# Layer-norm state updated in place, and the last residual add moved from VectorE to GpSimd

## The chip, the core and the metric

The program runs on one core of one Trainium2 chip. The metric is the device time of one execution in microseconds (us); lower is better. The engines are TensorE (PE in the profile), VectorE (DVE), ScalarE (ACT), GpSimd (POOL) and SyncE (SP), which issues most of the transfers. Each engine runs its own instruction list in order, and lists meet only at semaphores.

## The reference, cut to what matters

One decoder layer with layer norm after each residual, float32, on x of shape (8, 128, 256) and a context of the same shape:

```python
x = layernorm(x + attention(x, Wq, Wk, Wv, Wo))          # 16 heads of 128, 4 key/value heads, rotary
x = layernorm(x + long_convolution(ctx, ctx, x, kernel, D))  # pair products of ctx, convolved, times x
x = layernorm(x + gated_attention(x, W_gate, W_qkv))     # 16 heads of 16, top-1 gate picks k and v
```

All three norms are `(x - mean) / sqrt(var + 1e-5)` over the 256 features, with no weights.

## The kernel before, in words

The 8 sequences of 128 tokens each live in SBUF as `x[128, 8, 256]`, one token per partition. The program has two phases.

**Phase A** runs the first attention and the convolutions, in 8 units of four heads and half of the sequences. It ends with `accumulate`, which adds the attention's output into `x`. All of phase A but its last unit is the same in both kernels.

**Phase B** handles the sequences one after another in turns `b = 0..7` (`seq` for turns 0 to 3, `last_seq` for turns 4 to 7; each engine has its own version with a hand-written order). The turns are software-pipelined: turn `b` finishes the third stage of sequence `b`, while it prepares sequences `b + 1` to `b + 4`. The steps that matter here, for one sequence:

- `first_apply` (DVE, L1187) normalises `x[:, b, :]` after the first attention. It writes `x1[:, j, :]`, a ring of two buffers (`j = b % 2`) laid over `v_tok`. PE turns it (`x1_turn`, L550) and ACT copies it to `qmix` (`mix_query`, L862).
- POOL multiplies it with the convolved pairs (`products`, L300 and L303), DVE sums (`mix_sum`, L1219), PE turns the sum back (`mix_turn`, L560), and `add_mix` (DVE, L1225) adds it to `x1`.
- The second norm: `norm_stats` (L1194), `norm_aggr` (L1199), `norm_eps` (L1203) on DVE, the power -1/2 on POOL (`second_power`, L1494), and `second_apply` (DVE, L1208), which writes `x2[:, j, :]`, a second ring over `v_tok`.
- PE turns `x2` (`x2_turn`, L568), and ACT runs `keep_x2` (L871), a copy of `x2[:, j, :]` into `x[:, b, :]`, because the ring will be overwritten before the last stage needs it.
- The third stage: gate (`gating`, `share`), keys spread over four blocks (`block_keys_hi` on ACT, `block_keys` on POOL, L1484 and L1487), scores (`fscores`, L615 to L617), row maximum (`frow_max`, DVE, L1283), exponentials (`fexps`, ACT, L912), turned probabilities (`fturn`, L625; `fprob_copy`, L919), and the product with the values (`fvalues`, L636), in four chunks `c = 0..3` of four heads.
- `y_invert` and `y_scale` (DVE, L1294, L1298) divide by the row sums, `add_ffn` (DVE, L1305) adds the residual `x[:, b, :]` to `y_flat`, and the third norm follows: `norm_stats(1, ...)`, `norm_aggr`, `norm_eps` on DVE, the power on POOL, `norm_apply` on DVE (L1208, into `x[:, b, :]`), and SP stores the row.

The order on DVE around the change, in turns 0 to 3, is: `y_scale(b)`, `norm_eps` of the second norm of sequence `b+3`, `add_ffn(b)`, `norm_stats(1, b)`, `frow_max(b+1, 2)`, `norm_aggr(1, b)`, `second_apply(b+3)`, `norm_eps(1, b)`, `query_lo(b+2)`, `norm_apply(1, b)`. On POOL it is: both halves of `products(b+4)`, `second_power(b+3)`, `block_keys(b+2)`, and the power of the third norm of `b`.

Of the kernel before, what the change touches and what calls it, by code (L numbers as in the profile page):

```python
# [21 lines left out]
P = 128  # L22
NB = 8
D = 256
# [29 lines left out]
def decoder_kernel(nc, xt_d, x_d, wqkv_d, wo_d, toep_d, dcoef_d, ctx_d, wf_d, cos_d, sin_d, ident_d,  # L54
                   anti_d, causal_d, blocks_d, ties_d, out_d):
    ctx = ExitStack()
    with ctx:
# [65 lines left out]
        mixT = t_cos[:, :, 0:D]  # L123
        x1 = v_tok[:, :, 0:D]
        x2 = v_tok[:, :, D:2 * D]
        x2T = k_rope[:, :, 0:D]
# [84 lines left out]
        x2T_done = sem("x2T_done")  # L211
        x2_kept = sem("x2_kept")
        x2copy_done = sem("x2copy_done")
# [132 lines left out]
        def _(pe):  # L346
# [195 lines left out]
            def x1_turn(b, j):  # L542

                pe.wait_ge(ln1[4], b + 1)
                if isinstance(b, int) and b == 1:
                    pe.wait_ge(qmix_done, 1)
                else:
                    at_least(pe, x2copy_done, b, 2)
                for c in range(C):
                    last = pe.transpose(mix_bank[:, c * P:(c + 1) * P], x1[:, j, c * P:(c + 1) * P],  # L550
                                        ident[:, :])
                last.then_inc(x1T_done, 1)
# [11 lines left out]
            def x2_turn(b, j):  # L564

                pe.wait_ge(ln2[5], b + 1)
                for c in range(C):
                    last = pe.transpose(mix_bank[:, c * P:(c + 1) * P], x2[:, j, c * P:(c + 1) * P],  # L568
                                        ident[:, :])
                last.then_inc(x2T_done, 1)  # L570
# [149 lines left out]
        def _(act):  # L720
# [146 lines left out]

            def keep_x2(b, j):

                act.wait_ge(ln2[5], b + 1)  # L870
                act.copy(x[:, b, :], x2[:, j, :]).then_inc(x2_kept, 1)  # L871

            def gate_copy(b):
# [50 lines left out]
            x2_copy(0, 0)  # L924
            keep_x2(0, 0)
            gate_copy(0)
# [6 lines left out]
            mix_query(3, 1)  # L933
            keep_x2(1, 1)
            gate_copy(1)
# [7 lines left out]
            def seq(b, j):  # L943
# [4 lines left out]
                mix_query(b + 4, j)  # L948
                keep_x2(b + 2, j)
                fexps(b, 3)  # L950
# [10 lines left out]
            def last_seq(b, j):  # L961
# [12 lines left out]
                if b + 2 < NB:  # L974
                    gate_exp(b + 2)
                    keep_x2(b + 2, j)
                fprob_copy(b, 3)
# [12 lines left out]
        def _(dve):  # L990
# [73 lines left out]
            def unit(v, j, has_next, has_more):  # L1064
# [31 lines left out]
                if not has_next:  # L1096
# [21 lines left out]
                    add_mix(0, 0)  # L1118
                    norm_stats(0, ln2, 0, x1[:, 0, :])
                    norm_aggr(0, ln2, 0)  # L1120
# [62 lines left out]
            def first_apply(b, j):  # L1183

                dve.wait_ge(ln1[3], b // BH + 1 if isinstance(b, int) else NS)
                at_least(dve, ln2[5], b, 2)
                dve.tensor_scalar(x1[:, j, :], x[:, b, :], mean_var1[:, b, 0:1], rstd1[:, bass.ds(b, 1)],  # L1187
                                  ALU.subtract, ALU.mult).then_inc(ln1[4], 1)
# [22 lines left out]
            def second_apply(b, j):  # L1211
                at_least(dve, x2_kept, b, 2)
                norm_apply(0, ln2, b, x1[:, j, :], x2[:, j, :])

# [7 lines left out]
            def add_mix(b, j):  # L1222
                dve.wait_ge(mix_done, b + 1)
                dve.wait_ge(ln1[4], b + 1)
                dve.tensor_tensor(x1[:, j, :], mix_bank[:, 0:D], x1[:, j, :], ALU.add).then_inc(ln2[0], 1)  # L1225

            def mix_norm(b, j):
                add_mix(b, j)
                norm_stats(0, ln2, b, x1[:, j, :])
                norm_aggr(0, ln2, b)  # L1230
                norm_eps(0, ln2, b)
                second_apply(b, j)
# [68 lines left out]

            def add_ffn(b):
                dve.wait_ge(ynorm_done, b + 1)
                dve.wait_ge(x2_kept, b + 1)
                dve.tensor_tensor(y_flat, y_flat, x[:, b, :],  # L1305
                                  ALU.add).then_inc(ln3[0], 1)

            phase_a(dve, unit)
# [4 lines left out]
            add_mix(1, 1)  # L1313
            norm_stats(0, ln2, 1, x1[:, 1, :])
            norm_aggr(0, ln2, 1)
# [14 lines left out]
            def seq(b, j):  # L1330
# [7 lines left out]
                add_mix(b + 3, 1 - j)  # L1338
                norm_stats(0, ln2, b + 3, x1[:, 1 - j, :])
                y_invert(b)  # L1340
                norm_aggr(0, ln2, b + 3)
                y_scale(b)
                norm_eps(0, ln2, b + 3)
                add_ffn(b)
                norm_stats(1, ln3, b, y_flat)
# [7 lines left out]
            def last_seq(b, j):  # L1353
# [13 lines left out]
                if b + 3 < NB:  # L1367
                    add_mix(b + 3, 1 - j)
                    norm_stats(0, ln2, b + 3, x1[:, 1 - j, :])
                if b + 1 < NB:  # L1370
# [5 lines left out]
                if b + 3 < NB:  # L1376
                    norm_eps(0, ln2, b + 3)
                add_ffn(b)
                norm_stats(1, ln3, b, y_flat)
# [11 lines left out]
        def _(pool):  # L1391
# [88 lines left out]
            def block_keys(b, j):  # L1480
# [8 lines left out]
                                   mask, ALU.mult).then_inc(kblock_lo_done, 1)  # L1489

            def power(dst, src, ln, count):

# [20 lines left out]
            def seq(b, j):  # L1513
                products(b + 4, j, NEAR)
                products(b + 4, j, FAR)
                second_power(b + 3)
                block_keys(b + 2, j)
                power(rstd_of[1][:, :], var_eps_of[1][:, :], ln3, b + 1)

            def last_seq(b, j):  # L1520
                if b + 3 < NB:
                    second_power(b + 3)
                if b + 2 < NB:
                    block_keys(b + 2, j)
# [57 lines left out]
```

## Time and profile before

| | |
|---|---|
| median of 3 runs | 372.49 us (372.28 to 373.48) |
| the profiled execution | 370.43 us, of which the span from first to last instruction is 368.5 us |
| PE, DVE, ACT, POOL busy over the span | 88%, 74%, 61%, 56% |
| mean granted clock of TensorE | 0.968 of full speed |
| phase B | from about 245 us to the end |

The busy shares are means over both phases. In the rows below, a line of a timeline gives start, duration, engine, source line, operation, output and inputs with their shapes, and in brackets how long the engine sat idle before it and what ended that. Consecutive instructions of an engine may overlap slightly, because decoding and draining are pipelined.

### The profile page before, as it was taken

The page shows a single profiled execution, that of the slowest core. Times are in us where ns is not written, and L with a number is a line of the kernel's source. Part 1 is how long each engine was busy: PE and PEld are TensorE (multiplying, and loading weights), DVE is VectorE, ACT ScalarE, POOL GpSimd, SP SyncE. Part 2 cuts the span into 40 slices and gives each one's busy share as a digit, 9 for nine tenths or more (in the row PEclk, how much of TensorE's full clock was granted, in tenths as well). Part 3 has the DMA queues.
Part 4 walks back from the last instruction along what each step waited for, and adds up shares of the span by engine and source line. Part 5 has one row for each costly group of instructions (what it writes and reads, how often), then busy time and mean ns, then how long its engine had stood idle before and what let it go on. Part 6 is the DMA issues. An engine that isn't in the chain of part 4 may idle for free.

```text
span 368.5 us, 5868 instructions
## 1 busy us (share of the span) xinstructions
PE 325.6 (88%) x1912; PEld 257.9 (70%) x1912; DVE 274.5 (74%) x527; ACT 226.3 (61%) x703; POOL 207.5 (56%) x291
## 2 busy tenths in 40 slices
PE   1958899999999999999999999673889999999993
PEld 0745778788778788778788788552477767777783
DVE  2774966955966955966955956988889999998662
ACT  4548567666567666667666655322467687688772
POOL 0488654756754756753756752885948767822200
PEclk9989999999999999999999999997789999999996
DMA  7911000031010031000040000000000000000000
GB/s 258 343 54 57 4 28 2 1 116 57 1 30 0 3 114 59 1 28 2 0 126 0 2 2 0 3 0 0 0 4 0 16 14 1 18 16 14 0 16 28
DMA packets 5757, 13.05 MB, mean 35 GB/s; under 512 B 992, under 2 KB 3168, under 8 KB 5472
## 3 DMA queue, kind: packets, MB, share of 16 engines
q1 hardware_dynamic: 5184, 11.90, 9.5%
q10 hardware_dynamic: 544, 0.79, 0.7%
q8 instruction: 15, 0.25, 0.2%
q14 instruction: 14, 0.11, 0.1%
HBM read 11.63 MB, written 1.05 MB: 34 GB/s over the span
## 4 chain that ended last, share of the span: by engine, by line
PE 61%; DVE 25%; issue 8%; ACT 2%; POOL 2%; DMA 1%; POOLq 0%; DVEq 0%; ACTq 0%
PE bank L357 13%; PE bank L478 12%; PE bank L388 8%; PE bank L374 7%; PE bank L467 5%; PE bank L456 3%; DVE toep L1029 3%; PE bank L636 3%; DVE t_cos L1219 2%; DVE neg_max L1283 2%; DMA x_raw<-in_xt 1%; PE bank L625 1%; PE bank L584 1%; DVE t_cos L996 1%; DVE v_tok L1208 1%
## 5 line engine op out<-in xcount | busy, mean ns | idle before, releaser
L1431 POOL TENSOR_TENSOR prob<-prob,rden 128x512 f32<-128x512 f32 x32 | 33.5, 1047 | 72.3 <-DVE rden L1056 72.3
L1410 POOL TENSOR_TENSOR t_sin<-rot,sin 128x512 f32<-128x512 f32 x40 | 54.3, 1359 | 27.4 <-ACT rot L752 24.7
L776 ACT ACTIVATE prob<-bank,neg_max 128x128 f32<-128x128 f32 x128 | 45.4, 368 | 39.2 <-DVE neg_max L1049 39.1
L357 PE MATMUL bank<-x_hi,w_hi 128*128 128x512 f32 x96 | 37.2, 470 | 8.6 <-ACT w_hi L733 8.1
L912 ACT ACTIVATE prob<-bank,neg_max 128x128 f32<-128x128 f32 x128 | 36.8, 375 | 11.7 <-DVE neg_max L1283 11.3
L388 PEld LDWEIGHTS bank<-k_rope,q_rope 128*128 128x128 f32 x256 | 34.6, 198 | 10.3 <-DVE q_rope L1009 4.9
L478 PE MATMUL bank<-wo_hi,head_hi 128*128 128x256 f32 x128 | 39.0, 304 | 3.0 <-DVE head_lo L1083 3.0
L388 PE MATMUL bank<-k_rope,q_rope 128*128 128x128 f32 x256 | 35.1, 282 | 4.5 <-DVE q_rope L1009 4.5
L300 POOL TENSOR_TENSOR q_rope<-y,rot 128x128 f32<-128x128 f32 (+7 forms) x60 | 31.4, 530 | 10.2 <-ACT rot L862 10.2
L478 PE MATMUL bank<-wo_lo,head_hi 128*128 128x256 f32 x128 | 36.1, 282 | 0.0
L478 PE MATMUL bank<-wo_hi,head_lo 128*128 128x256 f32 x128 | 36.1, 282 | 0.0
L636 PEld LDWEIGHTS bank<-vext,probT 128*128 128x128 f32 x256 | 33.2, 198 | 3.1 <-issue 2.9
L1400 POOL TENSOR_TENSOR kv<-ctxT 128x256 f32<-128x256 f32 (+3 forms) x64 | 35.3, 585 | 0.0
L374 PE MATMUL bank<-kv,toep 128*128 128x288 f32 x96 | 29.1, 414 | 5.8 <-DVE t_cos L996 5.8
L751 ACT COPY rot<-bank 64x512 f32<-64x512 f32 x40 | 23.4, 584 | 17.3 <-PE bank L357 16.4
L1083 DVE TENSOR_TENSOR head_lo<-bank,head_hi 128x512 fp32r<-128x512 f32 x32 | 21.9, 686 | 15.4 <-ACT head_hi L816 15.4
L467 PE MATMUL bank<-probT,v_tok 128*128 128x512 f32 x64 | 33.2, 600 | 0.0
L1494 POOL TENSOR_TENSOR rstd<-var_eps,half_pow 128x1 f32<-128x1 f32 (+1 forms) x18 | 11.6, 644 | 37.8 <-DVE var_eps L1203 36.8
L636 PE MATMUL bank<-vext,probT 128*128 128x17 f32 x256 | 32.0, 258 | 0.0
L357 PE MATMUL bank<-x_hi,w_lo 128*128 128x512 f32 x96 | 30.9, 403 | 0.0
L1009 DVE TENSOR_TENSOR q_rope<-t_cos,t_sin 128x512 f32<-128x512 f32 x32 | 30.0, 941 | 1.1
L357 PE MATMUL bank<-x_lo,w_hi 128*128 128x512 f32 x96 | 30.8, 402 | 0.0
(106 smaller groups left out, 813.5 us busy)
## 6 DMA issues: line engine op xcount, KB each, us to landing
w_raw<-in_wqkv SPq DMA_DIRECT2D x3, 768.0 KB, 4.9
toep<-in_toep SPq DMA_DIRECT2D x8, 256.0 KB, 3.2
wo_raw<-in_wo SPq DMA_DIRECT2D x4, 512.0 KB, 3.5
x_raw<-in_xt SPq DMA_DIRECT2D x2, 512.0 KB, 6.1
ctxT<-in_ctx SPq DMA_DIRECT2D x1, 1024.0 KB, 9.0
x<-in_x SPq DMA_DIRECT2D x1, 1024.0 KB, 10.2
out<-x SPq DMA_DIRECT2D x8, 128.0 KB, 1.7
wf<-in_wf SPq DMA_DIRECT2D x1, 784.0 KB, 4.6
```

What stands on the lines that cost most here:

```text
L300: last = eng.tensor_tensor(pr[:, :, d * HD:d * HD + (n - 1) * (HD + 1) + 1:HD + 1], y[:, :, at:at + n], q[:, :, 0:n], ALU.mult)
L357: last = pe.matmul(out[:, :], wp[:, c, col:col + P], xp[:, j, c, :], start=(c + n == 0), stop=(c == C - 1 and n == 2))
L374: last = pe.matmul(out, toep[:, j, hh, tap:tap + P], kv[:, j, m, hh * NB:(hh + 1) * NB, :], start=(m == 0), stop=(m == lb))
L388: last = pe.matmul(score_bank[k % 2][:, h * P:(h + 1) * P], q_rope[:, j, h, k * P:(k + 1) * P], k_rope[:, j, k * P:(k + 1) * P], start=Tru ...
L467: pe.matmul(headT_bank[:, :], v_tok[:, j, k * P:(k + 1) * P], probT[:, k % 2, :], start=True, stop=True).then_inc(pv_done, 1)
L478: last = pe.matmul(acc_bank[k // 2][:, (k % 2) * D:(k % 2 + 1) * D], hp[:, k % 2, h * P:(h + 1) * P], wp[:, 4 * v + h, :], start=(h + n == ...
L636: last = pe.matmul(y_bank[:, f * (FD + 1):(f + 1) * (FD + 1)], probT[:, c % 2, h * P:(h + 1) * P], vext[:, b, :], start=True, stop=True)
L776: last = act.activation(prob[:, k % 2, h * P:(h + 1) * P], score_bank[k % 2][:, h * P:(h + 1) * P], ACT.Exp, bias=neg_max[:, k % 2, h:h + ...
L912: last = act.activation(prob[:, c % 2, h * P:(h + 1) * P], fscore_bank[c % 2][:, h * P:(h + 1) * P], ACT.Exp, bias=neg_max[:, c % 2, h:h + 1])
L1400: last = pool.tensor_tensor(kv[:, buf, :, :, at:at + n], src[:, :, :, 0:n], src[:, :, :, d:HD], ALU.mult)
L1410: pool.tensor_tensor(t_sin[:, par, :].rearrange("p (b t) -> p b t", b=BH), rot[:, par, :].rearrange("p (b t) -> p b t", b=BH), sin[:, :].u ...
L1431: pool.tensor_tensor(own, own, rden[:, k % 2, :].unsqueeze(2).to_broadcast([P, HG, P]), ALU.mult).then_inc(norm_done, 1)
```

## The change

The two rings `x1` and `x2` go away. `first_apply`, `add_mix` and `second_apply` all read and write `x[:, b, :]` in place; the two waits that protected the rings go with them. `keep_x2` on ACT and its semaphore are removed. `add_ffn` leaves DVE and becomes a GpSimd instruction; it stands on POOL between `second_power(b+3)` and `block_keys(b+2)`. DVE's next instruction for sequence `b`, `norm_stats(1, b)`, waits as before for `ln3[0]`, which POOL now signals.

```diff
-        x1 = v_tok[:, :, 0:D]
-        x2 = v_tok[:, :, D:2 * D]
...
             def first_apply(b, j):
                 dve.wait_ge(ln1[3], b // BH + 1 if isinstance(b, int) else NS)
-                at_least(dve, ln2[5], b, 2)
-                dve.tensor_scalar(x1[:, j, :], x[:, b, :], mean_var1[:, b, 0:1], rstd1[:, bass.ds(b, 1)],
+                dve.tensor_scalar(x[:, b, :], x[:, b, :], mean_var1[:, b, 0:1], rstd1[:, bass.ds(b, 1)],
                                   ALU.subtract, ALU.mult).then_inc(ln1[4], 1)
...
             def second_apply(b, j):
-                at_least(dve, x2_kept, b, 2)
-                norm_apply(0, ln2, b, x1[:, j, :], x2[:, j, :])
+                norm_apply(0, ln2, b, x[:, b, :], x[:, b, :])
...
-                dve.tensor_tensor(x1[:, j, :], mix_bank[:, 0:D], x1[:, j, :], ALU.add).then_inc(ln2[0], 1)
+                dve.tensor_tensor(x[:, b, :], mix_bank[:, 0:D], x[:, b, :], ALU.add).then_inc(ln2[0], 1)
...
-            def keep_x2(b, j):                      # ACT; its 8 calls go too
-
-                act.wait_ge(ln2[5], b + 1)
-                act.copy(x[:, b, :], x2[:, j, :]).then_inc(x2_kept, 1)
...
-            def add_ffn(b):                         # DVE; its calls in seq and last_seq go too
-                dve.wait_ge(ynorm_done, b + 1)
-                dve.wait_ge(x2_kept, b + 1)
-                dve.tensor_tensor(y_flat, y_flat, x[:, b, :],
-                                  ALU.add).then_inc(ln3[0], 1)
...
+            def add_ffn(b):                         # POOL
+                pool.wait_ge(ynorm_done, b + 1)
+                pool.wait_ge(ln2[5], b + 1)
+                y_flat = ynorm[:, :, :].rearrange("p h d -> p (h d)")
+                pool.tensor_tensor(y_flat, y_flat, x[:, b, :], ALU.add).then_inc(ln3[0], 1)
...
                 second_power(b + 3)                 # POOL, seq; the same place in last_seq
+                add_ffn(b)
                 block_keys(b + 2, j)
                 power(rstd_of[1][:, :], var_eps_of[1][:, :], ln3, b + 1)
```

`x1_turn`, `x2_turn` and `norm_stats` read `x[:, b, :]` in place of the rings; nothing else differs.

## Rows read from the trace of the kernel before

**Rows 1.** Windows: us, then busy of PE, PEld, DVE, ACT, POOL; clock, DMA

```profile
282.46:295.52 13.06, 12.50 (x83) 9.51 (x83) 12.71 (x32) 9.81 (x35) 9.65 (x19) 1.00 0.03 11
...
335.49:347.96 12.47, 11.77 (x81) 9.11 (x80) 8.69 (x25) 9.70 (x33) 4.19 (x6) 1.00 0.03 11
```

**Rows 2.** Timeline, DVE in turn 1, around the residual add

```profile
295.04 0.42 DVE L1298 TENSOR_TENSOR x_raw<-bank,yden 128x256 f32<-128x256 f32 x1
...
295.38 0.14 DVE L1203 TENSOR_SCALAR var_eps<-mean_var 128x1 f32<-128x1 f32 x1
...
295.50 0.42 DVE L1305 TENSOR_TENSOR x_raw<-x_raw,x 128x256 f32<-128x256 f32 x1
...
295.96 0.43 DVE L1194 BATCH_NORM_STATS2 stats<-x_raw 128x6 f32<-128x256 f32 x1
...
296.30 0.67 DVE L1283 TENSOR_REDUCE neg_max<-bank 128x4 f32<-128x512 f32 x1
...
296.99 1.02 DVE L1208 TENSOR_SCALAR v_tok<-v_tok,mean_var,rstd 128x256 f32<-128x256 f32 x1
```

**Rows 3.** Timeline, POOL in turn 1, the same stretch

```profile
295.60 0.72 POOL L1494 TENSOR_TENSOR rstd<-var_eps,half_pow 128x1 f32<-128x1 f32 x1 [1.03 <-DVE var_eps L1203]
...
296.30 0.45 POOL L1484 TENSOR_TENSOR ksT_lo<-x_raw,ksT_hi 128x128 fp32r<-128x128 f32 x1
...
296.83 1.04 POOL L1487 TENSOR_TENSOR x_hi<-ksT_lo,blocks 128x512 fp32r<-128x512 f32 x1
```

**Rows 4.** Source line of the copy that goes: min/median/max ns

```profile
L871 ACT COPY x<-v_tok x8: 388/410/466, 244.8 to 341.4; 128x256 f32<-128x256 f32 x8
```

**Rows 5.** Timeline, ACT in turn 1

```profile
297.88 1.14 ACT L912 ACTIVATE prob<-bank,neg_max 128x128 f32<-128x128 f32 x4
```

**Rows 6.** Groups by form, POOL: busy us, mean ns of one

```profile
L1425 POOL TENSOR_TENSOR wo_lo<-wo_raw,wo_hi 128x1024 fp32r<-128x1024 f32 x4 | 9.5, 2382 | 0.0
L1400 POOL TENSOR_TENSOR kv<-ctxT 128x256 f32<-128x256 f32 x8 | 8.5, 1062 | 0.0
...
L1400 POOL TENSOR_TENSOR kv<-ctxT 128x224 f32<-128x224 f32 x8 | 4.9, 612 | 0.0
```

**Rows 7.** Groups by form, POOL in phase B

```profile
L300 POOL TENSOR_TENSOR q_rope<-y,rot 128x256 f32<-128x256 f32 x7 | 5.2, 748 | 10.2 <-ACT rot L862 10.2
...
L1484 POOL TENSOR_TENSOR ksT_lo<-x_raw,ksT_hi 128x128 fp32r<-128x128 f32 x8 | 3.6, 455 | 9.9 <-ACT ksT_hi L897 9.9
```

**Rows 8.** Timeline, the end: power on POOL, then apply on DVE

```profile
365.39 0.54 POOL L1494 TENSOR_TENSOR rstd<-var_eps,half_pow 128x1 f32<-128x1 f32 x1 [6.38 <-DVE var_eps L1203]
365.97 0.41 DVE L1208 TENSOR_SCALAR x<-x_raw,mean_var,rstd 128x256 f32<-128x256 f32 x1 [0.66 <-POOL rstd L1494]
```

**Rows 9.** Timeline, turn 4: DVE, POOL and PE

```profile
335.34 0.14 DVE L1203 TENSOR_SCALAR var_eps<-mean_var 128x1 f32<-128x1 f32 x1
...
335.92 0.43 DVE L1194 BATCH_NORM_STATS2 stats<-x_raw 128x6 f32<-128x256 f32 x1
...
336.48 0.40 DVE L1208 TENSOR_SCALAR v_tok<-v_tok,mean_var,rstd 128x256 f32<-128x256 f32 x1
...
336.79 1.04 POOL L1487 TENSOR_TENSOR x_hi<-ksT_lo,blocks 128x512 fp32r<-128x512 f32 x1
...
336.94 0.44 PE L568 MATMUL bank<-ident,v_tok 128*128 128x128 f32 x2
```

**Rows 10.** Timeline, turns 5 and 6: DVE, ACT and PE

```profile
347.50 0.43 DVE L1298 TENSOR_TENSOR x_raw<-bank,yden 128x256 f32<-128x256 f32 x1
...
350.60 0.47 PE L615 MATMUL bank<-x_hi,w_hi 128*128 128x512 f32 x1
...
350.90 1.15 ACT L912 ACTIVATE prob<-bank,neg_max 128x128 f32<-128x128 f32 x4 [0.29 <-DVE neg_max L1283]
...
352.19 0.63 PE L625 MATMUL bank<-ident,prob 128*128 128x128 f32 x4
...
359.02 1.14 ACT L912 ACTIVATE prob<-bank,neg_max 128x128 f32<-128x128 f32 x4 [1.13 <-DVE neg_max L1283]
```

More of the change, by code:

```diff
@@ L211, in decoder_kernel @@
         x2T_done = sem("x2T_done")
-        x2_kept = sem("x2_kept")
         x2copy_done = sem("x2copy_done")
@@ L549, in x1_turn @@
                 for c in range(C):
-                    last = pe.transpose(mix_bank[:, c * P:(c + 1) * P], x1[:, j, c * P:(c + 1) * P],
+                    last = pe.transpose(mix_bank[:, c * P:(c + 1) * P], x[:, b, c * P:(c + 1) * P],
                                         ident[:, :])
@@ L567, in x2_turn @@
                 for c in range(C):
-                    last = pe.transpose(mix_bank[:, c * P:(c + 1) * P], x2[:, j, c * P:(c + 1) * P],
+                    last = pe.transpose(mix_bank[:, c * P:(c + 1) * P], x[:, b, c * P:(c + 1) * P],
                                         ident[:, :])
@@ L924, in _ @@
             x2_copy(0, 0)
-            keep_x2(0, 0)
             gate_copy(0)
@@ L933, in _ @@
             mix_query(3, 1)
-            keep_x2(1, 1)
             gate_copy(1)
@@ L948, in seq @@
                 mix_query(b + 4, j)
-                keep_x2(b + 2, j)
                 fexps(b, 3)
@@ L975, in last_seq @@
                     gate_exp(b + 2)
-                    keep_x2(b + 2, j)
                 fprob_copy(b, 3)
@@ L1118, in unit @@
                     add_mix(0, 0)
-                    norm_stats(0, ln2, 0, x1[:, 0, :])
+                    norm_stats(0, ln2, 0, x[:, 0, :])
                     norm_aggr(0, ln2, 0)
@@ L1224, in add_mix @@
                 dve.wait_ge(ln1[4], b + 1)
-                dve.tensor_tensor(x1[:, j, :], mix_bank[:, 0:D], x1[:, j, :], ALU.add).then_inc(ln2[0], 1)
+                dve.tensor_tensor(x[:, b, :], mix_bank[:, 0:D], x[:, b, :], ALU.add).then_inc(ln2[0], 1)
             def mix_norm(b, j):
                 add_mix(b, j)
-                norm_stats(0, ln2, b, x1[:, j, :])
+                norm_stats(0, ln2, b, x[:, b, :])
                 norm_aggr(0, ln2, b)
@@ L1313, in _ @@
             add_mix(1, 1)
-            norm_stats(0, ln2, 1, x1[:, 1, :])
+            norm_stats(0, ln2, 1, x[:, 1, :])
             norm_aggr(0, ln2, 1)
@@ L1338, in seq @@
                 add_mix(b + 3, 1 - j)
-                norm_stats(0, ln2, b + 3, x1[:, 1 - j, :])
+                norm_stats(0, ln2, b + 3, x[:, b + 3, :])
                 y_invert(b)
@@ L1343, in seq @@
                 norm_eps(0, ln2, b + 3)
-                add_ffn(b)
                 norm_stats(1, ln3, b, y_flat)
@@ L1368, in last_seq @@
                     add_mix(b + 3, 1 - j)
-                    norm_stats(0, ln2, b + 3, x1[:, 1 - j, :])
+                    norm_stats(0, ln2, b + 3, x[:, b + 3, :])
                 if b + 1 < NB:
@@ L1377, in last_seq @@
                     norm_eps(0, ln2, b + 3)
-                add_ffn(b)
                 norm_stats(1, ln3, b, y_flat)
@@ L1522, in last_seq @@
                     second_power(b + 3)
+                add_ffn(b)
                 if b + 2 < NB:
```

## The prediction

> **What bounds the kernel now.** I read the page's shares first: PE is busiest over the whole span. That is a mean over two phases, and the change touches phase B alone, so I cut phase B into turns, each from one residual add to the next, and read the windows. In turn 0 (13.06 us, and turns 1 to 3 look the same) DVE is busy 12.71 us, ACT 9.81, POOL 9.65 [rows 1]. PE shows 12.50, but its records overlap and it waits for DVE's normalised rows. The chain of waits, followed back through these turns, runs almost without a break along DVE. So in turns 0 to 3 a microsecond added to DVE's list is a microsecond on the end, and one removed there counts just as fully. In turn 4 (12.47 us) DVE is busy only 8.69 us and PE 11.77 [rows 1]: there the path is PE's, and what counts of DVE is the moment at which it hands PE the next rows. In turns 5 to 7 the path goes round PE, DVE and ACT.
>
> Then I read the timeline around the add in turn 1, which stands for turns 0 to 3. DVE runs the scaling, `norm_eps` (295.38), the add (295.50, 0.42 us), the statistics (295.96), the row maximum (296.30), and `second_apply` (296.99), back to back [rows 2]. POOL runs the power (295.60) and the two instructions of `block_keys` (296.30 and 296.83) [rows 3]. What the reader is to see is that `second_apply` takes 1.02 us there and 0.40 us in turn 4 [rows 2, 9]. In turn 1 it starts 0.16 us after the 1.04 us `kblock` instruction of POOL and ends at 298.01, 0.14 us after POOL's end at 297.87 [rows 2, 3]. In turn 4 it starts 0.31 us ahead of `kblock` and is not held [rows 9]. One of the two holds the other out for its whole length.
>
> **The change part by part.**
>
> *The ACT copies.* Eight of 0.41 us go, 3.3 us of ACT's work [rows 4]. In turns 0 to 3 the copy stands in ACT's list ahead of the exponentials of chunk 3, but what they feed reaches DVE, which has no idle to give up. In turns 4 and 5 it stands ahead of instructions that wait for DVE's maximum. The source line lists nobody waiting for it. Value: 0. If DVE were not the bound of turns 0 to 3, up to 0.41 us a turn would come back, 1.6 us.
>
> *The two ring waits on DVE and the in-place writes.* The waits concern work that ended a turn earlier; shapes and operands stay in SBUF with the same sizes. Value: 0, between a gain of a few hundredths a turn and nothing.
>
> *The add leaves DVE.* Its slot, start of the add to start of the statistics, is 295.50 to 295.96: 0.46 us a turn [rows 2]. That is the gain if the sum were ready in time.
>
> *The add on POOL.* Its own price must be bounded, since no such add of 128x256 with two full SBUF inputs is in the trace of POOL without disturbance. Low: 0.61 us, the 128x224 pair product [rows 6]. A line from 128x128 (455 ns [rows 7]) to the 512 columns of `kblock` (1.04 us [rows 3]) gives 0.65 at 256; a line from 455 ns to 2382 ns at 1024 columns [rows 6] gives 0.455 + 128 x 0.00215 = 0.73; the product of the same size is 0.748 [rows 7]. High: 1.06 us, the 128x256 pair product [rows 6]. I take 0.70, in the middle of the three nearest.
>
> The Trainium skill ("GPSIMD Engine Reference", section "Elementwise — side-by-side cycle accounting") puts GpSimd at 1.96 times DVE for an add of 2048 float32 columns. By that the add would take 0.83 us as an estimate, and the sum below would be about 1.0 us higher; the rows of POOL itself lie lower, and I go by them.
>
> *The new wait.* `norm_stats(1, b)` is now DVE's next instruction after `norm_eps`, so DVE stands still until POOL is done, and behind it stand the row maximum of `b+1`, `second_apply(b+3)`, `query_lo` and the output's `norm_apply`. POOL cannot start at once: the power of sequence `b+3` stands ahead of it and starts only after `norm_eps`. In turn 1: power starts 295.60, and takes 0.54 us when DVE is quiet, as at the end [rows 8], rather than 0.72 beside DVE's add [rows 3]. POOL's next instruction starts 0.02 before that end, as 296.30 against 295.60 + 0.72 [rows 3]: 296.12. The add ends 296.82. DVE follows 0.04 after a POOL end (365.93 to 365.97 [rows 8]): statistics at 296.86 instead of 295.96. DVE's row maximum is 0.90 late.
>
> *What of the 0.90 reaches the path.* `second_apply` would be ready at 296.86 + 1.03 = 297.89. `kblock` now starts at 296.80 + 0.53 = 297.33 and ends 298.37, so DVE is again held, and ends 0.14 later, 298.51 instead of 298.01: 0.50 late. The old hold-up absorbs 0.40 of the stall. The late row maximum (296.97 + 0.90 = 297.87) is just in time for ACT, which starts those exponentials at 297.88 [rows 5], and POOL's later blocks are needed only in the next turn. Turns 0 to 3: 4 x 0.50 = 2.0 us.
>
> The Trainium skill ("SBUF — State Buffer", section "Who interferes with whom") describes such a hold as an exclusive lock on a port pair that DVE and GpSimd share; taken by a two-port DVE instruction or one with two SBUF inputs, and by whoever starts first. The 1.02 and the 0.72 us above agree with it. Without any such lock `second_apply` would end at 298.30, and these turns would cost 4 x 0.29 = 1.2 us.
>
> *Turn 4.* `norm_eps` starts 335.34, so the power starts 335.56, the add 336.08 (as above, 0.22 and 0.52 on), its end is 336.78. No row maximum stands between statistics and `second_apply` here: it came 0.56 after the statistics (335.92 to 336.48 [rows 9]), so it is ready at 337.38. `kblock` starts at 336.76 + 0.53 = 337.29, 0.09 earlier, and the order of before is reversed: `second_apply` waits and ends 338.47 instead of 336.88. That is 1.59 us, and PE's `x2_turn` started right behind it (336.94 [rows 9]) with the path on it. If DVE still came first, it would be 337.78, 0.90 late. I take 1.59 by the order of the starts, and keep 0.90.
>
> *Turns 5 to 7.* No power stands ahead. From the end of the scaling to the statistics it was 0.50 us (295.46 to 295.96 [rows 2]); it becomes 0.08 (DVE to POOL, as 295.52 to 295.60 [rows 2, 3]) + 0.70 + 0.04 = 0.82: 0.32 late each. In turn 5 it reaches the exponentials, whose end 352.05 stood 0.14 ahead of PE's use at 352.19 [rows 10]: 0.18. In turn 6 it stands ahead of the last row maximum, for which ACT waits 1.13 us and starts at 359.02 [rows 10]: 0.32 in full. In turn 7 everything is one chain: 0.32. Together 0.82. `block_keys(7)` now waits behind the add of turn 5: scaling ends 347.93, add 348.71, `kblock` 350.26, still 0.34 ahead of the scores that read it at 350.60 [rows 10]; if it were later, PE would wait for the difference.
>
> *Sum.* 2.0 + 1.59 + 0.82 - 0 = 4.4 us. The profiled execution goes from 370.43 (span 368.5, 1.9 us around it) to 374.8. The median stands 2.06 us above the profiled time; with it the forecast is 372.49 + 4.4 = 376.9 us, 1.2% slower.
>
> **Rivals.**
>
> *A, a smaller loss.* DVE wins the start in turn 4 (less 0.7), and the add costs 0.61 (less 0.09 x 8 = 0.7): 3.0 us, 375.5; with no hold-up in turns 0 to 3 besides (less 0.8), 2.2 us, 374.7. For it: 0.09 us decides turn 4. Against: the two nearest forms are dearer than 0.61.
>
> *B, a larger loss.* The add takes 1.06 us on POOL: 0.36 x 8 = 2.9 us more, 7.3 us, 379.8. For it: the row exists, with two full inputs. Against: it was taken beside a busy DVE, and here DVE stands still. If the add stays at 0.70 but the late row maximum makes ACT and PE late too, so that nothing is absorbed, it is 4 x 0.40 more: 6.0 us, 378.5. ACT had 0.01 us to spare.
>
> *C, DVE is relieved (the other side).* The bound engine loses 0.46 us a turn: 8 x 0.46 = 3.7 us faster, 368.8. It needs the sum to be ready when the statistics want it, so the add would have to end within 0.5 us of the scaling. It decides from that point. For it: DVE is 97% busy in these turns. Against: the power alone takes 0.54 us ahead of the add. The Trainium skill ("Perfetto Trace Analysis", section "Optimizing Scalar/DVE Operations") says that where DVE is saturated, offloading to Scalar or even GPSIMD may make sense, and doubts it for the shared port; here the order of the lists is the stronger doubt.
>
> *D, no difference.* The stall is absorbed whole: DVE has slack in turns 0 to 3 after all, or the freed ACT time (1.6 us) and a short add cancel it. About 372.5.
>
> **How the numbers follow.** The measurement can tell about 0.3%, 1.1 us. The forecast 0.52, A 0.22, B 0.15, C 0.04, D 0.07. The range takes in A and the most of B: 374.0 to 379.5. Faster 0.04; same 0.07; slower 0.89.
>
> **What the profile after would show.** DVE's `norm_stats` of the third norm idle before it some 1.3 us in turns 0 to 4 and about 0.8 in 5 to 7, released by POOL's add; the power at 0.54 instead of 0.72; turns 0 to 3 about 13.6 us long; `second_apply` in turns 0 to 3 shorter, about 0.6 us, and in turn 4 about 1.1 instead of 0.40. The forecast is wrong if the turns stay at 13.1 us, if the add is far from 0.70, or if `second_apply` in turn 4 goes ahead of `kblock`.

## The result, and the profile after

| | before, same chip | changed |
|---|---|---|
| median | 372.38 us (4 runs, 371.22 to 373.48) | 380.56 us (4 runs, 378.64 to 383.31) |
| ratio | | 1.0226, 95% interval 1.0144 to 1.0307 |
| the profiled execution | 370.43 us, span 368.5 | 379.0 us, span 377.2 |

The changed kernel is 8.2 us slower by the medians and 8.7 us by the profiled spans. The forecast was +4.4 us, and 380.56 lies above the range of 374.0 to 379.5. The same kernel measured again on another chip (run e5 below) gave 380.01 us, ratio 1.0251 [1.0208, 1.0294].

A warning for every number below: executions of one and the same kernel differ by several us, because TensorE's clock does not fall in the same places in each. The kernel before took between 368.3 us (mean granted clock 0.975) and 378.6 us (0.943). So medians carry the verdicts and single traces carry the mechanism. A ratio leaves out the executions that are on record as slow (those over 1.5% above their kernel's fastest) and a median does not, so a ratio is not always the quotient of the two medians beside it.

First the timeline of turn 1 in the changed kernel, on DVE and then on POOL; it answers to [rows 2, 3].

```profile
295.51 0.42 DVE L1284 TENSOR_TENSOR x_raw<-bank,yden 128x256 f32<-128x256 f32 x1
295.85 0.14 DVE L1190 TENSOR_SCALAR var_eps<-mean_var 128x1 f32<-128x1 f32 x1
297.36 0.43 DVE L1181 BATCH_NORM_STATS2 stats<-x_raw 128x6 f32<-128x256 f32 x1 [1.36 <-POOL x_raw L1473]
297.70 0.67 DVE L1269 TENSOR_REDUCE neg_max<-bank 128x4 f32<-128x512 f32 x1
...
298.39 0.62 DVE L1195 TENSOR_SCALAR x<-x,mean_var,rstd 128x256 f32<-128x256 f32 x1
```

```profile
296.07 0.55 POOL L1478 TENSOR_TENSOR rstd<-var_eps,half_pow 128x1 f32<-128x1 f32 x1 [1.03 <-DVE var_eps L1190]
296.59 0.73 POOL L1473 TENSOR_TENSOR x_raw<-x_raw,x 128x256 f32<-128x256 f32 x1
297.28 0.46 POOL L1462 TENSOR_TENSOR ksT_lo<-x_raw,ksT_hi 128x128 fp32r<-128x128 f32 x1
297.82 1.04 POOL L1465 TENSOR_TENSOR x_hi<-ksT_lo,blocks 128x512 fp32r<-128x512 f32 x1
```

The add has left DVE, and DVE's statistics now stand 1.36 us idle until POOL's add ends. POOL runs the power first, then the add. From the scaling's start to the statistics it was 0.92 us and is 1.85. `second_apply` (L1195) still overlaps the `kblock` instruction (L1465), but is held for only 0.62 us instead of 1.02, so it ends 3.50 us after the scaling's start instead of 2.97. That is 0.53 us later; 0.50 was forecast.

Now the windows of the changed kernel, one for each turn 0 to 6, from scaling to scaling. The columns are those of [rows 1].

```profile
281.91:295.51 13.60, 12.76 (x85) 9.66 (x84) 11.92 (x31) 9.59 (x34) 10.20 (x20) 1.00 0.03 11
295.51:309.11 13.60, 12.54 (x84) 9.56 (x83) 11.92 (x32) 9.74 (x34) 10.19 (x20) 1.00 0.03 10
309.11:322.71 13.60, 12.54 (x84) 9.57 (x83) 11.92 (x32) 9.74 (x34) 10.20 (x20) 1.00 0.04 13
322.71:336.81 14.10, 12.70 (x86) 9.86 (x86) 11.77 (x32) 11.24 (x40) 3.26 (x5) 1.00 0.03 10
336.81:355.82 19.01, 16.70 (x81) 12.59 (x81) 9.03 (x26) 9.70 (x34) 3.25 (x5) 0.73 0.02 7
355.82:365.21 9.39, 9.21 (x71) 7.84 (x71) 5.40 (x13) 7.80 (x26) 2.70 (x4) 1.00 0.05 16
365.21:371.91 6.70, 5.37 (x45) 4.84 (x43) 2.45 (x8) 3.46 (x11) 1.28 (x2) 0.99 0.06 20
```

Before, the same turns cut in the same way took 13.07, 13.17, 13.20, 13.59, 12.50, 9.13 and 6.92 us, and from the last scaling to the end of DVE's list it was 2.83 us against 3.17 after. The row to look at is that of turn 4: 19.01 us instead of 12.50, with a granted clock of 0.73 instead of 1.00. The timeline of turn 4 of the changed kernel, with DVE, POOL and PE, answers to [rows 9]:

```profile
338.65 0.43 DVE L1181 BATCH_NORM_STATS2 stats<-x_raw 128x6 f32<-128x256 f32 x1 [1.36 <-POOL x_raw L1473]
...
339.11 1.04 POOL L1465 TENSOR_TENSOR x_hi<-ksT_lo,blocks 128x512 fp32r<-128x512 f32 x1
...
339.22 1.08 DVE L1195 TENSOR_SCALAR x<-x,mean_var,rstd 128x256 f32<-128x256 f32 x1
...
340.36 0.44 PE L565 MATMUL bank<-ident,x 128*128 128x128 f32 x2 [1.76 <-DVE x L1195]
...
348.66 3.16 PE L581 MATMUL bank<-wf,k_rope 128*128 128x512 f32 x4
```

And the windows over the stretch behind that wait, first of the changed kernel, then of the one before:

```profile
338.00:341.00 3.00, 1.24 (x9) 0.74 (x8) 2.26 (x7) 2.06 (x7) 2.62 (x4) 1.00 0.00 0
341.00:346.00 5.00, 5.00 (x23) 4.39 (x23) 2.77 (x8) 2.86 (x11) 0.00 (x0) 0.50 0.08 26
346.00:351.00 5.00, 5.00 (x13) 3.06 (x14) 0.79 (x2) 2.20 (x8) 0.00 (x0) 0.50 0.00 0
351.00:354.00 3.00, 2.44 (x16) 1.75 (x15) 1.78 (x5) 0.00 (x0) 0.00 (x0) 0.96 0.00 0
```

```profile
338.00:341.00 3.00, 3.00 (x26) 2.70 (x26) 2.23 (x6) 2.79 (x12) 0.33 (x1) 1.00 0.13 44
341.00:346.00 5.00, 4.44 (x24) 2.68 (x24) 2.71 (x7) 2.84 (x12) 0.00 (x0) 1.00 0.00 0
346.00:351.00 5.00, 4.90 (x39) 4.35 (x38) 4.20 (x12) 4.28 (x14) 2.04 (x3) 1.00 0.00 0
```

PE stood still for 1.76 us, waiting for `second_apply`. Right behind, from about 341.0 to 351.2 us, TensorE runs at the lower of its two levels, 1.2 GHz instead of 2.4. The four 512-column matmuls of L581 start there and take 3.16 us (2.6 us of it at the lower level, the rest behind 351.2); at full clock, in the kernel before, the same four took 1.88 us:

```profile
341.62 1.88 PE L584 MATMUL bank<-wf,k_rope 128*128 128x512 f32 x4
```

The account of the 8.70 us of span, from these rows: turns 0 to 3, +1.87; turn 4, +1.61 because `second_apply` ends 3.49 us after the scaling's start instead of 1.88; turn 4 again, 19.01 - 12.50 - 1.61 = **+4.90 from the clock**; turn 5, +0.26; turn 6, +0.36 against the 6.34 us that it takes without a loss of clock (traces of e4 and e13), less the 0.58 us that the clock had cost it before (6.92 - 6.34); turn 7, +0.34; the start of turn 0, -0.06. The waits alone are 1.87 + 1.61 + 0.26 + 0.36 + 0.34 = 4.4 us. The 4.90 us agree with the length of the slow stretch: matmuls that take twice their time for 10.2 us lose 5.1 us, if PE is what bounds the turn.

### The profile page after: what moved, and what is told of

Same layout as the page of the kernel before. It is cut to its first block, busy times and chain, and to the rows that moved or that the text cites. A ratio compares the mean times of both kernels' runs of the same rounds, so it can differ in the third digit from the quotient of the medians.

```text
span 377.2 us, 5848 instructions
## 1 busy us (share of the span) xinstructions
PE 329.5 (87%) x1912; PEld 260.6 (69%) x1912; DVE 269.9 (72%) x519; ACT 224.6 (60%) x695; POOL 212.3 (56%) x299
## 2 busy tenths in 40 slices
DMA packets 5757, 13.05 MB, mean 35 GB/s; under 512 B 992, under 2 KB 3168, under 8 KB 5472
## 3 DMA queue, kind: packets, MB, share of 16 engines
HBM read 11.63 MB, written 1.05 MB: 34 GB/s over the span
## 4 chain that ended last, share of the span: by engine, by line
PE 59%; DVE 16%; POOL 11%; issue 8%; ACT 3%; DMA 2%; POOLq 0%; DVEq 0%; ACTq 0%
PE bank L354 13%; PE bank L475 12%; PE bank L385 7%; PE bank L371 7%; PE bank L464 5%; POOL q_rope L297 4%; PE bank L453 3%; POOL q_rope L300 3%; DVE toep L1017 3%; PE bank L633 3%; DMA w_raw<-in_wqkv 2%; PE bank L622 2%; POOL x_raw L1473 2%; DVE t_cos L984 1%; PE bank L581 1%
## 5 line engine op out<-in xcount | busy, mean ns | idle before, releaser
L1269 DVE TENSOR_REDUCE neg_max<-bank 128x4 f32<-128x512 f32 x32 | 22.0, 686 | 10.8 <-PE bank L614 10.6
```

## The experiments

Theories. **T1**: the waits are worth what the forecast said, and the rest is TensorE's clock, lost because PE stood still in turn 4. Rivals: **R1**, the in-place half (readers and writers of `x` collide) costs part of it; **R2**, POOL's work itself slows the others; **R3**, the fall of the clock is chance or comes from elsewhere. Turns are counted as in the windows above, from DVE's scaling; PE's list runs one turn ahead of that, so the `x2_turn` for which PE waits in turn 4 stands in PE's turn `b = 5`. Executions differ in number, n. The time before is that of the same chip.

### Which half: e1, e2, and the change again (e5)

e1 keeps the state in place, with the add back on DVE. e2 keeps rings and ACT copies, with the add on POOL.

```diff
 # e1, against the changed kernel            # e2, against the kernel before
-add_ffn(b)    (POOL)                        -add_ffn(b)    (DVE)
+add_ffn(b)    (DVE, before norm_stats)      +add_ffn(b)    (POOL, after second_power)
```

> The in-place half alone: rings and ACT copies gone, the add still on DVE. Theory (the whole loss comes from the add on POOL): 372.4 us within 0.3% of the kernel before, turns 0 to 3 still 13.1 to 13.2 us. Rival (the in-place writes or the freed ACT time matter): over 1.1 us away from the kernel before.

> The other half alone: rings and ACT copies kept, the add on POOL behind the power. Theory: as the changed kernel, 379 to 383 us, with the same 1.36 us wait before the third norm's statistics and TensorE's granted clock at 0.50 for about 10 us after turn 4. Rival (the halves work together): under 377 us, or no stretch at 0.50.

> The changed kernel itself once more, for a second trace and more times beside those of the next three on the same chip. Theory (waits worth 4.4 us, and a PE wait of 1.76 us in turn 4 after which the clock falls in most executions): turns 0 to 3 of 13.6 us again; turn 4 19.0 us with the clock at 0.50, or 14.1 us where it stays at 1.00; median 7 to 10 us above the kernel before, with a scatter of some 4 us. Rival (the long turn 4 was an accident of one profile): turn 4 of 14.1 us and a median within 5 us of the kernel before.

| | this | before | ratio | turns 0 to 3, 4 |
|---|---|---|---|---|
| e1 | 371.84 (n = 10) | 370.99 | 0.9994 [0.9949, 1.0040] | 13.05 13.13 13.13 13.58, 12.46 |
| e2 | 381.06 (n = 4) | 370.99 | 1.0289 [1.0257, 1.0321] | 13.56 13.56 13.58 14.11, 19.03 |
| e5 | 380.01 (n = 6) | 371.94 | 1.0251 [1.0208, 1.0294] | 13.57 13.57 13.57 14.09, 17.34 |

The whole loss is in the moved add. The eight ACT copies, the two waits and the writes in place are worth nothing that can be measured (e1, to within 0.5%), so R1 falls. In e2 the clock is 0.50 from 342.6 to 352.8, in e5 from 345.1 to 352.0, both behind a PE wait of 1.75 us.

### Is it the clock: PE kept busy in the wait (e3, e6)

Matmuls on constants into a free bank of PSUM stand in PE's list ahead of the `x2_turn` of turn 4; their result is not used. e3 has four, e6 two.

```diff
+                if b + 2 == NB - 1:
+                    pe.wait_ge(masked_done, NB - 1)
+                    for _ in range(4):                   # e6: 2
+                        pe.matmul(kvf_bank[:, :], ident[:, :], wf[:, 0, D:3 * D], start=True, stop=True)
                 if b + 2 < NB:
                     x2_turn(b + 2, j)
```

> The changed kernel with four extra matmuls of 128x512 whose result nobody reads, put on PE into the 1.76 us in which it waits for second_apply in turn 4. Theory (PE's idleness lowers its clock, and that costs 4.9 us): the stall on DVE stays, the clock stays at 1.00 through turns 4 and 5, and the profiled time falls by 4 to 5 us, to about 374.5. Rival (the lost time is the stall itself passed down a longer chain, or the clock falls for another reason): no change or up to 0.5 us slower, and the stretch at 0.50 stays.

> The changed kernel with two extra float32 matmuls of 128x512 in PE's wait of turn 4 (two passes each, together about 1.7 us, so that they fit the wait of 1.76 us). Theory (the idle PE is what lets the clock fall): turn 4 is 14.1 us with the clock at 1.00, and the median is 3 to 5 us below the changed kernel of the same call. Rival (the clock falls by chance, whatever PE does in turn 4): turn 4 of 19 us as often as in the changed kernel, medians equal within 1 us.

The timeline of PE in e3:

```profile
340.28 3.60 PE L691 MATMUL bank<-wf,ident 128*128 128x512 f32 x8
343.71 0.38 PE L565 MATMUL bank<-ident,x 128*128 128x128 f32 x2
```

Each float32 matmul of 512 columns ran as two records, 0.45 us apiece, so e3's four took 3.60 us and overshot the wait: turn 4 takes 15.56 us, all at clock 1.00, and the kernel 378.74 us (before 370.99; 1.0209 [1.0158, 1.0260]), where about 374.5 was expected. e6 fits: turn 4 takes 14.10 us at clock 1.00, which is 12.50 + 1.60, and the kernel takes 377.13 us (before 371.94; 1.0175 [1.0131, 1.0219], n = 6). Work added to a kernel made it 380.0 - 377.1 = 2.9 us faster on the same chip (e5 against e6), and five of e6's six executions are faster than the fastest of e5. That is what T1 says, and R3 does not. e6 is still 5.2 us above before rather than 4.4. Its profiled execution lost clock in turns 0 and 1 as well (16.63 and 14.98 us), so for the traces e3 is the fairer comparison: the clock last rose 61.3 us before the place of the wait there, 61.7 us in e5; e3's clock stayed and e5's fell.

### Is a late hand-over enough: e4, e11, e12, e13

The kernel before, with nothing moved to POOL. DVE gets statistics over a constant tile, ahead of `second_apply`, so that it comes late.

```diff
+                if b == NB - 4:                         # turn 4
+                    for i in range(5):                  # e4 and e11: 5; e12: 1
+                        dve.bn_stats(pad_stats[:, i, :], pad[:, :])
                 second_apply(b + 3, 1 - j)
 # e13: 5 in turn 4, and 3 in each of turns 0 to 3
```

> The kernel before, with nothing on POOL changed, and five bn_stats of a constant put on DVE ahead of second_apply in turn 4, so that it is about 1.7 us late there and nowhere else. Theory (a PE wait of about 1.8 us in turn 4 costs itself plus some 4.9 us at the lower clock): about 372.4 + 1.7 + 4.9 = 379 us. Rival (only a chain through POOL can do it): 374.1 us, clock 1.00.

> The kernel before with second_apply of turn 4 late by 1.6 us through DVE, once more: its first trace kept the clock at 1.00 in turn 4 (14.1 us), while two of its four times were 3.7 us and more above the other two. Theory (the wait makes a fall likely, not certain): this trace or some of the times show it; median 3 to 5 us above the kernel before. Rival (the fall needs POOL's add): all times within 2.5 us of the kernel before, apart from as many outliers as that has.

> The kernel before with one bn_stats on DVE ahead of second_apply in turn 4, so that it starts just behind kblock's start and ends about 1.1 us late; PE's wait there becomes about 1.2 us. Theory: turn 4 of 13.6 us; median 1.1 us above the kernel before if a wait of 1.2 us leaves the clock alone, 4 us or more if it does not. Rival (a held second_apply costs less than its delay): turn 4 under 13.0 us.

> The kernel before, with DVE alone made late: three bn_stats of a constant ahead of second_apply in turns 0 to 3 (0.5 us late behind kblock, PE's wait 0.7 us instead of 0.17), five in turn 4 (PE's wait 1.76 us). Theory (the small waits of turns 0 to 3 and the large one of turn 4 together lower the clock, whoever makes them): turns 0 to 3 about 13.6 us, turn 4 17 to 19 us with the clock at 0.50, 8 us above the kernel before. Rival (it needs POOL's add): turn 4 of 14.1 us at 1.00, 3.5 us above.

| | this | before | ratio | PE wait | turn 4, clock |
|---|---|---|---|---|---|
| e4 | 376.22 (n = 4) | 370.99 | 1.0143 [1.0081, 1.0205] | 1.76 | 14.12, 1.00 |
| e11 | 373.64 (n = 12) | 371.84 | 1.0040 [1.0001, 1.0080] | 1.76 | 14.11, 1.00 |
| e12 | 373.23 (n = 12) | 371.84 | 1.0036 [0.9996, 1.0075] | 1.24 | 13.58, 1.00 |
| e13 | 377.45 (n = 4) | 371.71 | 1.0178 [1.0108, 1.0249] | 1.76 | 17.37, 0.80 |

e4 and e11 miss what T1 expected of them (379 us, a fall of the clock) and go against its simple form: the same 1.76 us of PE wait in turn 4, and the clock stays. So a wait of that length is not enough. (The two are the same kernel on two chips; e4's profiled execution lost clock in turn 1 instead, 14.53 us, and the two medians, 5.2 and 1.8 us above before, show how little four executions can be trusted.) In e12 a shorter wait, 1.24 us, left the clock alone too. e13 shows that POOL is not needed either. With DVE's own work alone making turns 0 to 4 longer (13.39, 13.41, 13.38, 13.93), the same wait is followed by the fall, as in the windows of e13:

```profile
339.00:341.00 2.00, 1.95 (x16) 1.76 (x16) 1.89 (x5) 0.67 (x3) 0.54 (x1) 0.94 0.00 0
341.00:343.00 2.00, 2.00 (x10) 1.57 (x8) 0.89 (x3) 1.62 (x7) 0.00 (x0) 0.50 0.19 66
```

R2 falls with it as the cause of the fall. e13 is 5.7 us above before, where 8 was expected: its slow stretch is 6.8 us long instead of 10.2, and its turns 5 to 7 have no added wait. What is left is that something in the turns ahead decides, besides the wait in turn 4.

### Which turns: e9, e10, e14, e15

The changed kernel with the add on POOL in some turns only, and on DVE in the others.

```diff
+                if b <= 4:                              # e15; e9: b < 4, e10: b >= 4, e14: b >= 3
                     add_ffn(b)                          # POOL; elsewhere DVE
```

> In place, with the add on POOL in turns 0 to 3 and on DVE in turns 4 to 7. Theory: turns 0 to 3 of 13.6 us, then 14.1 for turn 3 to 4; turn 4 of 12.5 us with no PE wait over 0.2 us and the clock at 1.00; 1.9 us above the kernel before. Rival (PE's waits of 0.68 us in turns 0 to 3 already let the clock fall in turn 4 or in these turns): over 4 us above it.

> In place, with the add on DVE in turns 0 to 3 and on POOL in turns 4 to 7. Theory: waits worth 1.6 + 3 x 0.3 = 2.5 us, and the clock falls in turn 4 in most executions for 3 to 5 us more: 5 to 8 us above the kernel before. Rival (without the lighter PE load of turns 0 to 3 the same wait of 1.76 us leaves the clock at 1.00): 2.5 us above it, turn 4 of 14.1 us.

> In place, with the add on POOL in turns 3 to 7 and on DVE in turns 0 to 2. If the small PE wait nearest to the large one is what counts: turn 4 of 17 to 19 us with the clock at 0.50. If all four small waits count: turn 4 of 14.1 us at 1.00, 3.0 us above the kernel before.

> In place, with the add on POOL in turns 0 to 4 and on DVE in turns 5 to 7. Theory: as the changed kernel up to turn 4 (17 to 19 us, clock 0.50), and 0.9 us less behind it; 7 us above the kernel before. Rival (the later turns have a part in it): turn 4 of 14.1 us.

| | this | before | ratio | PE wait, turn 4 | turn 4, clock |
|---|---|---|---|---|---|
| e9 | 373.62 (n = 12) | 371.84 | 1.0013 [0.9970, 1.0055] | none | 12.48, 1.00 |
| e10 | 372.85 (n = 12) | 371.84 | 1.0058 [1.0025, 1.0091] | 1.75 | 14.10, 1.00 |
| e14 | 376.66 (n = 10) | 371.71 | 1.0098 [1.0052, 1.0143] | 1.75 | 14.09, 1.00 |
| e15 | 379.46 (n = 4) | 371.71 | 1.0237 [1.0195, 1.0279] | 1.76 | 19.03, 0.73 |

The two halves e9 and e10 measure +0.13% and +0.58% by the ratios, and 1.8 and 1.0 us by the medians, far short of the +2.5% or 8.1 us of both together: the loss is not a sum over turns. e15 has it whole, with the add on POOL in turns 0 to 4. Of these four kernels it alone has the longer turns 0 to 3 and the wait in turn 4 together. e9 against e15 is also the plainest test of the wait: the same turns 0 to 3, and the clock falls in turn 4 only where PE waits there. (e9's turns 0 to 3 are 1.8 us longer in its trace; its ratio shows 0.5 us of that, with an interval of 0.4% to either side. e14 and e10 differ by a turn of POOL adds, and by 0.4% in the ratio and 3.8 us in the median, which no trace explains: both traces lost clock ahead of turn 2, and three of e10's twelve executions and four of e14's ten took 378.0 us or more.)

The fall is not a throw of the dice in each execution either, as R3 would have it. All ten executions of the changed kernel took 378.6 us or more, and all eight of e2 and e15 379.4 or more, while nine of e10's twelve took 376.2 or less with the same wait.

### What about turns 0 to 3: small PE waits (e16) or the moment of the big one (e17, e18)

e16 puts one matmul of 256 columns into PE's small waits in `seq`. e17 adds one `bn_stats` behind `second_apply` in each of turns 0 to 3, e18 in turns 0 and 1: more work, meant to shift the moment at which turn 4 begins.

```diff
 # e16, in seq
+                pe.wait_ge(masked_done, b + 2)
+                pe.matmul(kvf_bank[:, 0:D], ident[:, :], wf[:, 0, D:2 * D], start=True, stop=True)
 # e17 (e18: b < 2)
+                if b < 4:
+                    dve.bn_stats(pad_stats[:, 0, :], pad[:, :])
```

> The changed kernel with one extra float32 matmul of 128x256 (two passes, about 0.43 us) in PE's wait of 0.68 us in each of turns 0 to 3, and nothing in turn 4. Theory (the small waits count too): turn 4 of 14.1 us with the clock at 1.00 in spite of its wait of 1.76 us, median near 377. Rival (only turn 4's wait counts and the three kernels that kept 1.00 were luck): turn 4 of 17 to 19 us.

> The changed kernel with one bn_stats of a constant on DVE behind second_apply in each of turns 0 to 3: 1.7 us more work, and PE's wait of 1.76 us in turn 4 comes 1.7 us later. In the six traces with a fall in turn 4 that wait began 61.6 or 64.8 to 65.9 us after the clock's last rise, in e11, which has none, 63.7 us after it. Theory (when the wait comes decides whether the clock falls): the wait comes 67.6 us after the rise, turn 4 is 14.1 us with the clock at 1.00, and the kernel is 3 us faster than the changed one in spite of more work. Rival (longer turns 0 to 3 are the condition): turn 4 of 17 to 19 us, and 1.7 us slower than the changed kernel.

> The same with the bn_stats in turns 0 and 1 alone: the wait comes 0.9 us later, some 66.7 us after the rise. If when it comes decides: either outcome, but not the same as e17's in every execution; turn 4 either 14.1 us or 15 to 19 us. If longer turns are the condition: turn 4 of 17 to 19 us, and 0.9 us slower than the changed kernel in the median.

e16: 379.01 us (before 371.71; 1.0217 [1.0162, 1.0272]), turn 4 19.01 us, clock 0.50 from 341.1 to 351.3. The small waits are not the condition, as far as they were filled: they shrank from 0.84 and 0.7 us to 0.39 and 0.25 in turns 0 to 2, and that of turn 3, 0.68 us, stayed. The expectation that filling them would keep the clock failed.

e17: 376.49 us (n = 4; before 371.39; 1.0128 [1.0089, 1.0168]). Its turns 0 to 3 are longer than in the changed kernel, 13.91, 13.90, 13.90 and 14.24 us, together +1.05; turn 4 takes 14.10 us. The timeline of PE and the window of turn 4 in e17:

```profile
346.17 0.44 PE L567 MATMUL bank<-ident,x 128*128 128x128 f32 x2 [1.75 <-DVE x L1198]
```

```profile
342.62:356.72 14.10, 11.79 (x81) 9.13 (x81) 9.02 (x25) 9.46 (x34) 3.25 (x5) 1.00 0.03 9
```

The same wait, the same instructions in the same turn, and no fall; so longer turns 0 to 3 together with the wait are not a sufficient condition. The changed kernel's ten executions took 378.6 us or more; three of e17's four took 375.1 to 376.8 with a microsecond more work in them (the profiled one, 381.5, lost clock elsewhere). But the trace is not the shift that was planned: the wait was to come 67.6 us after the clock's last rise and came 62.8 us after it, because in this execution the slow stretch ahead of turn 0 lasted 10.2 us instead of 3.4. e18, shifted by half as much, also kept the clock in turn 4 (14.09 us at 1.00) but took 376.1 to 394.7 us over four executions, 381.64 us at the median (before 371.39): its time decides nothing.

### Can the wait be made smaller: e7, e8

e7 is the changed kernel with POOL's add ahead of `second_power` in all turns. e8 is e1 with `second_apply` ahead of the row maximum in `seq`, to get it out of `kblock`'s way.

```diff
 # e7, POOL                                  # e8, DVE in seq
+                add_ffn(b)                  +                second_apply(b + 3, 1 - j)
                 second_power(b + 3)                          frow_max(b + 1, 2)
-                add_ffn(b)                                   norm_aggr(1, ln3, b)
                 block_keys(b + 2, j)        -                second_apply(b + 3, 1 - j)
```

> The changed kernel with the add ahead of the second norm's power in POOL's list. The third norm's statistics wait 0.8 us instead of 1.36. In turns 0 to 3 second_apply still meets POOL's kblock instruction at a start within 0.03 us of it: 13.6 us a turn if it is held, 12.8 if it goes first. In turn 4 it starts 0.4 us ahead of kblock and PE waits 0.5 us instead of 1.76. Theory: turn 4 12.9 us with the clock at 1.00; median 3 us above the kernel before if turns 0 to 3 are 13.6. Rival (it is the wait for the add, not who comes first at kblock, that sets turn 4): turn 4 13.5 us or more.

> The in-place kernel with the add on DVE, and second_apply moved ahead of the row maximum of the next sequence on DVE in turns 0 to 3, so that it starts 0.4 us before POOL's kblock instruction instead of 0.16 us after it. Theory (one of the two holds the other out for its whole length): second_apply 0.41 us instead of 1.02, turns 0 to 3 of 12.5 to 12.6 us instead of 13.1, 2.4 us faster than the kernel before. Rival (the 1.02 us has another cause, such as the busy memory): the turns stay at 13.1 us.

e7: 374.38 us (n = 12; before 371.94; 1.0078 [1.0046, 1.0111]), turns 13.51, 13.50, 13.50, 14.05 and 12.92, clock 1.00 in turn 4. The timeline of turn 1 in e7, DVE and `kblock`:

```profile
296.12 0.43 DVE L1181 BATCH_NORM_STATS2 stats<-x_raw 128x6 f32<-128x256 f32 x1 [0.78 <-POOL x_raw L1473]
...
297.09 1.04 POOL L1465 TENSOR_TENSOR x_hi<-ksT_lo,blocks 128x512 fp32r<-128x512 f32 x1
...
297.15 1.13 DVE L1195 TENSOR_SCALAR x<-x,mean_var,rstd 128x256 f32<-128x256 f32 x1
```

The wait shrinks from 1.36 to 0.78 us, but `second_apply` then comes 0.06 us behind `kblock` and is held for its whole length, 1.13 us; turns 0 to 3 gain only 0.05 to 0.10 us. In turn 4 the order turns: `second_apply` starts 337.73, `kblock` 338.13, and it takes 0.48 us. PE waits 0.57 us instead of 1.76.

e8: 372.20 us (n = 12; before 371.94; 1.0019 [0.9989, 1.0048]). `second_apply` takes 0.54 us in turn 1 instead of 1.02, yet the turns go only from 13.05, 13.13, 13.13, 13.58 to 13.00, 12.89, 12.99 and 13.51; 12.5 was expected. One row of DVE in e8 hints at what bounds next:

```profile
304.31 0.69 DVE L1250 TENSOR_TENSOR x_raw<-bank,chosen 128x512 f32<-128x512 f32 x1 [0.22 <-PE bank L581]
```

Here DVE waits for PE's key and value product. No kernel of this study beats the one before.

## Why the prediction was wrong

**The step that failed is the pricing of turn 4's hand-over.** The forecast said "1.59 us, and PE's `x2_turn` started right behind it [...] with the path on it", and put 1.59 into the sum. The delay was 1.61. But a late hand-over on PE's path is also a stop of PE, here 1.76 us, and the sum had no term for what TensorE's clock does behind it. It was worth 4.90 us in the profiled execution, more than all the waits together; without it the forecast sum of 4.4 us was right, with 1.87 + 1.61 + 0.96 us measured for 2.0 + 1.59 + 0.82. No rival had it: B reached 378.5 and 379.8 by a dearer add or an unabsorbed stall, and neither happened. The list of signs did not name the granted clock either. The trace of before had warnings of it ahead of turn 0, where PE is not yet always busy: PE stands still for 3.87 us until 254.5 and for 2.37 us until 267.8, and the clock is at 0.50 from 252.7 to 262.9 us and again from 269.7 to 273.1:

```profile
254.51 0.48 PE L604 MATMUL bank<-ident,x_raw 128*128 128x128 f32 x1 [3.87 <-DVE x_raw L1275]
...
267.84 0.33 PE L604 MATMUL bank<-ident,x_raw 128*128 128x128 f32 x1 [2.37 <-DVE x_raw L1275]
```

What supports the clock as the cause and not only as company: filling the wait with matmuls removes the slow stretch (e3, e6) and 2.9 us of the median (e6); leaving the wait out of turn 4 removes it, with turns 0 to 3 as in the changed kernel (e9 against e15); making the wait 0.57 us removes it (e7). e17, with 1.05 us of work added, has no fall in its trace and a median 3.5 to 4.1 us lower (380.01 and 380.56 to 376.49, on different chips); it fits, but its four executions and its unplanned clock make it the weakest of these.

What stays open is which stops cost the clock. In traces with a PE wait of 1.75 or 1.76 us in turn 4, one execution each, the clock fell in six (the changed kernel, e2, e5, e13, e15, e16), 2.3 to 3.5 us after the start of the wait, and stayed in six (e4, e10, e11, e14, e17, e18). In the six of the first kind the time from the last rise of the clock to the start of the wait was 61.7 to 66.0 us. But e11 (63.7) and e17 (62.8) lie inside that range and kept the clock, and e18 (66.1) stands next to it, so that distance alone is not the rule. The Trainium skill ("TensorE: Matmul & The Clock Gate", section "Part 1: The HAM clock gate (the "warmup" mystery)") says that the gate follows how busy PE has been, judged in windows that run free of the kernel. By that the same stop costs the clock or not according to where it falls, which agrees with six traces against six; no run here shows the windows themselves, and none placed the stop at a chosen moment.

**What held, point by point.**

- *The ACT copies, the ring waits, the writes in place: 0.* e1, ratio 0.9994.
- *The add on POOL: 0.70 us.* It took 0.722 to 0.734 us in eight instances, 0.03 above the forecast each time. Against the 0.42 us of DVE [rows 2] that is 1.7 times; by the 1.96 of the Trainium skill ("GPSIMD Engine Reference", section "Elementwise — side-by-side cycle accounting"), stated for 2048 columns, it would have been 0.83, an estimate. POOL's own rows were the better guide.
- *The new wait: 1.3 us in turns 0 to 4, 0.8 in 5 to 7.* 1.36 and 0.84. The power took 0.55 us once DVE stood still (0.54 forecast).
- *Turns 0 to 3: 2.0 us, since the old hold-up absorbs 0.40 of each stall.* 1.87. `second_apply` took 0.62 us (0.6 forecast). e7 shows the other side of the same hold: what one wait gives back, the hold takes.
- *Turn 4: the order of `kblock` and `second_apply` reverses.* It did, by 0.11 us (339.11 and 339.22), and `second_apply` took 1.08 us (forecast 1.1).
- *Turns 5 to 7: 0.82.* 0.26 + 0.36 + 0.34 = 0.96.
- *Rival C, DVE is relieved.* DVE's busy time in turn 1 fell from 12.82 to 11.92 us and the turn grew by 0.43. The order of the lists decided, not the load.

**A second step was too strong.** "One removed there counts just as fully": e8 freed 0.48 us a turn and got back 0.05 to 0.24. The other direction holds better, but not in full: the 0.41 us that e17 added to DVE in each of turns 0 to 3 made them 0.14 to 0.31 us longer than in the changed kernel. The next bound lies just below DVE's; in e8's row above it is PE.

## What to carry to other kernels

Moving an instruction from a saturated engine to a free one pays only if the result is there when the first engine's next instruction wants it; here 0.46 us of work became a 1.36 us wait, because a power stood ahead in the other list and the add is 1.7 times dearer there. And what the move gives the first engine can be lost on a third: here the late hand-over stopped TensorE. Where a change lets TensorE stand still in a stretch in which it was always busy, read the granted clock of that stretch, and price the stop twice: once as itself, and once with the matmuls of the following 7 to 10 us at half clock. The second price may or may not fall due, so it belongs into the range. If such a loss is suspected, fill the stop with matmuls that fit it, or make it shorter; a kernel that becomes faster with more work in it is strong evidence.

## What the runs showed of the hardware

- A stop of PE of 1.75 or 1.76 us between full stretches was followed by 6.8 us (e5, e13) or 10.2 us (the changed kernel, e2, e15, e16) at 1.2 GHz, though PE was busy without a break there (5.00 of 5.00 us in the two windows of the changed kernel above); it cost 3.2 us in e5 and 4.9 in the changed kernel. The same stop cost nothing in six other traces, and waits in the same place of 1.24 us (e12) and 0.57 us (e7) cost nothing in one trace each.
- `second_apply` on DVE and `kblock` on POOL hold each other out by the order of their starts: `second_apply` over 256 columns took 1.13 us when it started 0.06 us behind `kblock`, and 0.48 us when it started 0.40 us ahead of it (both e7).
